# Two reorderings of one kernel at once: the tokenizer's taps tile by tile, and the attention's turns, table and tail

## The reference

```python
# 1 tokenizer, per image: 7 x 7 patches, 192 channels
loc = dwconv(gelu(conv(x, pl_w, stride=16)))          # depthwise 3x3, then 1x1
g = gelu(dwconv(gelu(conv(wavelet_packet(x), pg_w1))))
h = (1 - gate) * loc + gate * conv(g, pg_w2)
h = relu(dwconv(h, f1)); h = relu(dwconv(h, f2)); h = dwconv(loc + h, f3)
t = concat([cls, layernorm(tokens(h))]); h = concat([t, txt], 1)   # 32 x 82 x 192
# 2 selective scan (mamba): rmsnorm, z and gate, scan of 16 states, W_out, gated FFN
h = h + mamba(layernorm(h))
# 3 attention and experts
x = layernorm(h); x2 = ln(x)
x = x + out_proj(softmax(q k^T / 4) v)                # 12 heads
xm = ln(x); probs = softmax(xm @ router_w)            # 8 experts, the best 2 of each token
for e in range(8): out += combine[:, e] * (gelu(xm @ w1[e] + b1[e]) @ w2[e] + b2[e])
h = h + x + out
```

## Time and profile before

| | us |
|---|---|
| runs, median (lowest to highest) | 1427.9 (1424.58 to 1437.63) |
| the profiled execution | 1429.09 |
| its span | 1427.3 |
| PE / DVE / ACT / POOL busy | 1210.3 / 1022.4 / 705.8 / 777.2 |
| mean granted clock of TensorE, 1 is 2.4 GHz | 0.917 |

### The profile page before, as it was taken

One profiled execution on the slowest core, in us unless ns is written; L12 is line 12 of the kernel. 1 busy time (PEld: TensorE's weight loads), 2 busy tenths in 40 slices (PEclk: granted clock), 3 DMA queues, 4 the chain that ended last, 5 costly groups with the idle time before them and its releaser, 6 DMA issues.

```text
span 1427.3 us, 19317 instructions
## 1 busy us (share of the span) xinstructions
PE 1210.3 (85%) x5756; PEld 783.2 (55%) x5757; DVE 1022.4 (72%) x1935; ACT 705.8 (49%) x1490; POOL 777.2 (54%) x499
## 2 busy tenths in 40 slices
PE   6895745485999989898987799999999799999996
PEld 4342223242454545454552468888878577777775
DVE  3699886798999999899999746677776663333232
ACT  1137642476868676767766245555541332222221
POOL 3037895479687888869697320134443465222322
PEclk9797655699999999999999999999996699999998
DMA  5200000342404040403220001122221133222221
GB/s 177 57 1 0 30 9 29 118 126 79 142 1 142 1 142 1 141 28 114 90 83 0 1 21 48 42 63 57 58 67 55 36 58 55 35 38 37 35 37 20
...
## 3 DMA queue, kind: packets, MB, share of 16 engines
...
q10 hardware_dynamic: 2184, 1.72, 0.5%
...
## 4 chain that ended last, share of the span: by engine, by line
PE 52%; DVE 23%; issue 8%; ACT 8%; POOL 5%; DMA 3%; DVEq 0%; SPq 0%; POOLq 0%; ACTq 0%
PE ps L2137 10%; PE ps L2156 6%; PE ps L961 6%; DVE hs L1244 6%; DVE ps L180 5%; PE ps L1616 3%; PE ps L1559 3%; PE ps L872 3%; PE ps L2146 2%; ACT ps L1114 2%; PE ps L1629 2%; PE ps L938 2%; PE ps L897 2%; PE ps L915 2%; PE ps L875 2%
## 5 line engine op out<-in xcount | busy, mean ns | idle before, releaser
L1362 POOL TENSOR_TENSOR Bx<-dtz,Bb 128x984 f32<-128x984 f32 x128 | 289.4, 2281 | 43.5 <-DVE hs L1244 29.9
L1244 DVE TENSOR_TENSOR_SCAN hs<-ps,Bx 128x492 f32<-128x492 f32 x256 | 287.6, 1164 | 22.1 <-POOL Bx L1362 12.7
L1114 ACT ACTIVATE ps<-dt,A 128x324 f32<-128x324 f32 (+1 forms) x512 | 211.5, 456 | 78.0 <-DVE hs L1244 77.2
L961 PE MATMUL ps<-hs,b_id 128*128 128x492 f32 x512 | 236.4, 584 | 12.0 <-DVE y L1211 9.3
L2256 POOL DMA_INDIRECT out<-yt,dest x48 | 74.8, 1558 | 164.7 <-DVE yt L2242 156.3
L1254 DVE TENSOR_TENSOR hs<-hs,ps 128x984 f32<-128x984 f32 x128 | 150.2, 1174 | 2.5 <-issue 0.6
L2137 PE MATMUL ps<-W,xT 97*128 (+1 forms) x384 | 140.6, 509 | 4.1 <-ACT hb L2194 1.4
L961 PEld LDWEIGHTS ps<-hs,b_id 128*128 128x128 f32 x512 | 92.2, 193 | 79.1 <-issue 73.8
L2226 DVE COPY hT__5781<-ps 128x768 f32<-128x768 f32 x48 | 46.0, 958 | 112.6 <-PE ps L2146 110.0
L2005 POOL DMA_INDIRECT buckets<-XS,c_slot x64 | 90.9, 1421 | 36.5 <-issue 23.6
L2012 POOL TENSOR_TENSOR c_x<-c_x,bro 82x192 f32<-82x192 f32 x32 | 19.2, 599 | 167.0 <-DVE c_x L1801 166.8
...
## 6 DMA issues: line engine op xcount, KB each, us to landing
...
```

The lines of the kernel that those rows point to most:

```text
L961: mm = pe.matmul(ps[:, BANK_Y + h, 0:HALF], ident[:], f2(hs[:, s % LONG])[:, h * HALF:(h + 1) * HALF], start=s == 0, stop=s == STATE - 1)
L1114: a = act.activation(ps[:, BANK_A + h, c:c + w].rearrange("p (g t) -> p g t", t=S)[:, :, 1:S], dt[:, (par + t // STATE) % 2, m, g0 * S:g1 ...
L1244: v.tensor_tensor_scan(f2(hs[:, t % LONG])[:, c], ps[:, BANK_A + h, 0:HALF], f2(Bx[:, t % RING])[:, c], 0.0, ALU.mult, ALU.add).then_inc(s ...
L1362: g.tensor_tensor(Bx[:, t % RING], dtz[:, p], Bb[:, p, t % STATE, :].rearrange("p (a n) -> p a n", a=1).broadcast_to([128, NI, N]), ALU.mu ...
```

## The change

Two changes, timed here together.

1. Tokenizer. `s_conv` and `s_gelu` count tiles; PE's next `conv` starts a tile as soon as its PSUM tile is free, ACT's Gelu and DVE's taps start with the first tile. The wait for D1 (and for the DF tiles) moves behind the eighth tap. On DVE the last waves are in another order; `third_sums` of the last chunk writes DF[0] rather than DF[2], and its ninth tap waits for the reader of DF[0] (`last_read`). On ACT the scan's piece of the last wave goes behind the last products, on POOL the roots go behind the two PF adds.
2. Attention. The turn of the normed rows moves from the end of q = 0 to q = 1, between scores and product with V; on DVE the attention's own small operations go ahead of `normed`, `rank` and `pick`; reading the counts (`offsets`) is first in q = 1. The first table covers 12 tiles and needs 4 rounds; it is made in round 6, in three parts, and no longer in the tail. In the tail PE turns tiles 0 and 1 ahead of the first step, `up` of tile 0 goes ahead of the second and of tile 1 ahead of the third. Two rounds' normed rows get buffers of their own, cleared early by POOL. The scatter-adds into the output have four buffers rather than two, and stand three to a round's scatters.

```diff
-        def dw(eng, own, src, dst, tiles, c, col, done):
+        def dw(eng, own, src, dst, tiles, c, col, done, given=None, read=None):
 
             part = src.shape[0]
             acc = psF[0:part, 0:ROWS * GRID].rearrange("p (r c) -> p r c", c=GRID)
             for k in tiles:
+                if given is not None:
+                    eng.wait_ge(*given(k))
                 for t in range(9):
+                    if t == 8 and read is not None:
+                        eng.wait_ge(*read(k))
...
+        def last_sums(c):
+            return DF[0] if c == CH - 1 else DF[2]
+
+        def last_read(c):
+            return (s_f[0], CH) if c == CH - 1 else (s_f[2], c * FILLS)
...
-                if c >= 1:
-                    pe.wait_ge(s_gelu, c)
                 for t in range(3):
+                    if c >= 1:
+                        pe.wait_ge(s_gelu, 3 * (c - 1) + t + 1)
                     for k in range(KT):
                         mm = pe.matmul(psC[:, t, 0:NP], wc[:, k, t * 128:(t + 1) * 128], xc[:, c % 2, k, :],
                                        start=k == 0, stop=k == KT - 1)
-                mm.then_inc(s_conv, 1)
+                    mm.then_inc(s_conv, 1)
...
-                act.wait_ge(s_conv, c + 1)
                 if c == 0:
                     act.wait_ge(s_pad, 1)
                     act.wait_ge(s_padp, 1)
                 for t in range(3):
-                    i = act.activation(padded(P1, t, c), psC[:, t, 0:NP].rearrange("p (i r c) -> p i r c", i=IM, r=GRID),
-                                       ACT.Gelu, bias=vec[:, V_CONV_B + t:V_CONV_B + t + 1])
-                i.then_inc(s_gelu, 1)
+                    act.wait_ge(s_conv, 3 * c + t + 1)
+                    act.activation(padded(P1, t, c), psC[:, t, 0:NP].rearrange("p (i r c) -> p i r c", i=IM, r=GRID),
+                                   ACT.Gelu, bias=vec[:, V_CONV_B + t:V_CONV_B + t + 1]).then_inc(s_gelu, 1)
...
-                if w == WAVES - 1:
-                    tail("last wave")
...
+                if w == WAVES - 1:
+                    tail("last wave")
...
-            for w in range(WAVES):
+            def local_sums(w):
+
+                dw(v, own, P1, D1, range(3), w, V_DW, s_dw1, given=lambda k: (s_gelu, 3 * w + k + 1),
+                   read=(lambda k: (s_loc, w) if k == 0 else (s_g, w)) if w > 0 else None)
+
+            def first_sums(c):
+
+                v.wait_ge(s_h, c + 1)
+                dw(v, own, PF[0], DF[0], (0,), c, V_F_DW, s_dwf[0], read=(lambda k: (s_f[0], c)) if c > 0 else None)
+
+            def second_sums(c):
+
+                v.wait_ge(s_r1, c + 1)
+                dw(v, own, PF[1], DF[1], (0,), c, V_F_DW + 18, s_dwf[1], read=(lambda k: (s_f[1], c)) if c > 0 else None)
+
+            def third_sums(c):
+
+                v.wait_ge(s_lr, c + 1)
+                dw(v, own, PF[2], last_sums(c), (0,), c, V_F_DW + 36, s_dwf[2], read=(lambda k: last_read(c)) if c > 0 else None)
+
+            for w in range(CH + 1):
                 if w < CH:
-                    v.wait_ge(s_gelu, w + 1)
-                    if w > 0:
-                        v.wait_ge(s_g, w)
-                    dw(v, own, P1, D1, range(3), w, V_DW, s_dw1)
-                if 0 <= w - 1 < CH:
-                    v.wait_ge(s_h, w)
-                    if w > 1:
-                        v.wait_ge(s_f[0], w - 1)
-                    dw(v, own, PF[0], DF[0], (0,), w - 1, V_F_DW, s_dwf[0])
-                if 0 <= w - 5:
-                    norm_rows(w - 5)
-                if 0 <= w - 4:
-                    take_rows(w - 4)
-                if w == WAVES - 1:
-                    tail("last taps")
-                if 0 <= w - 2 < CH:
-                    v.wait_ge(s_r1, w - 1)
-                    if w > 2:
-                        v.wait_ge(s_f[1], w - 2)
-                    dw(v, own, PF[1], DF[1], (0,), w - 2, V_F_DW + 18, s_dwf[1])
-                if w == WAVES - 2:
-                    tail("last but one taps")
-                if 0 <= w - 3 < CH:
-                    c = w - 3
-                    v.wait_ge(s_lr, c + 1)
-                    if c > 0:
-                        v.wait_ge(s_f[2], c * FILLS)
-                    dw(v, own, PF[2], DF[2], (0,), c, V_F_DW + 36, s_dwf[2])
+                    local_sums(w)
+                if w >= 1:
+                    first_sums(w - 1)
+                if w == CH:
+                    take_rows(0)
+                if w >= 2:
+                    second_sums(w - 2)
+                if w >= 3:
+                    third_sums(w - 3)
+            second_sums(CH - 1)
+            norm_rows(0)
+            take_rows(1)
+            tail("last but one taps")
+            third_sums(CH - 2)
+            norm_rows(1)
+            third_sums(CH - 1)
+            take_rows(CH - 2)
+            tail("last wave")
+            tail("last taps")
...
-                if 0 <= w - 4:
-                    roots(w - 4)
...
+                if 0 <= w - 4:
+                    roots(w - 4)
...
-FIRST = 16
-FULL_ROUNDS = 5
+FIRST = 12
+FULL_ROUNDS = 4
...
-            return XS[:, p % 2] if p < ROUNDS - 1 else XS_last[:]
+            if p in (ROUNDS - 3, ROUNDS - 1):
+                return XS_more[p // 2 - (ROUNDS - 3) // 2][:]
+            return XS[:, p % 2] if p < ROUNDS - 3 else XS[:, 1]
...
+            def normed_rows(i):
+                pe.wait_ge(s_xn, i - 2 + 1)
+                turn(slots(i - 2), ("NT0", "NT1"), s_nt, i)
+
             def route(i, par, q):
-                if q == 0 and is_round(i - 2):
-                    pe.wait_ge(s_xn, i - 2 + 1)
-                    turn(slots(i - 2), ("NT0", "NT1"), s_nt, i)
...
+                if q == 1 and is_round(i - 2):
+                    normed_rows(i)
...
             program(pe, step, front, route=route)
             i, par = ROUNDS, ROUNDS % 2
+            t = ex.tensor(pe)
+            pe.wait_ge(s_L, ROUNDS - 2)
+            t.turn(0, 0)
+            pe.wait_ge(s_sl, ROUNDS - 3)
+            t.turn(1, 1)
+            step(i, par, 0)
             pe.wait_ge(s_e, 32 * EXPERTS)
-            t = ex.tensor(pe)
-            step(i, par, 0)
-            route(i, par, 0)
-            pe.wait_ge(s_PTa, ROUNDS * G)
-            t.turn(0, 0)
-            step(i, par, 1)
-            route(i, par, 1)
-            t.turn(1, 1)
             pe.wait_ge(s_tab, 1)
             pe.wait_ge(s_E, ROUNDS * G)
             t.up(0, 0, t.expert(0))
+            pe.wait_ge(ex.s_xT, 2)
+            step(i, par, 1)
+            route(i, par, 1)
+            t.up(1, 1, t.expert(1))
             step(i, par, 2)
             pe.wait_ge(s_PTv, ROUNDS * G)
             pe.wait_ge(s_x3, ROUNDS * G - 1)
-            t.step(0, 0)
+            t.flip(0, 0)
+            pe.wait_ge(s_PTa, ROUNDS * G)
+            t.turn(2, 0)
             pe.wait_ge(s_x3, ROUNDS * G)
             t.step(1, 1)
-            route(i + 1, 1 - par, 0)
+            normed_rows(i + 1)
             prefix(ROUNDS - 2)
             t.step(2, 2)
             route(i + 1, 1 - par, 1)
...
-                if q == 0 and is_round(i - 2):
-                    normed(i - 2, par)
-                if q == 0 and is_round(i - 3):
-                    rank(i - 3)
-                if q == 2 and is_round(i - 2):
...
+                if q == 0 and is_round(i - 2):
+                    normed(i - 2, par)
+                if q == 0 and is_round(i - 3):
+                    rank(i - 3)
                 if q == 1 and is_round(i - 3):
+                    offsets(i - 3)
                     gates(i - 3)
                     place(i - 3)
+                if q == 2 and i < ROUNDS and is_round(i - 2):
+                    pick(i - 2)
+                if i == FULL_ROUNDS + 2:
+                    if q == 1:
+                        full_tiles()
+                    if q == 2:
+                        which_experts(0, FIRST, le_full)
+                    if q == 3:
+                        which_rows(0, FIRST, le_full, None)
...
-                if is_round(p - 2) and p < ROUNDS - 1:
-                    v.wait_ge(s_sc, (p - 1) * (16 * 2 * G))
+                if p in (ROUNDS - 3, ROUNDS - 1):
+                    v.wait_ge(s_pad, 1 if p == ROUNDS - 3 else 2)
+                elif is_round(p - 2):
+                    v.wait_ge(s_sc, min(p - 1, FULL_ROUNDS) * (16 * 2 * G))
...
             i, par = ROUNDS, ROUNDS % 2
             t = ex.vector(v)
             t.ones()
-            full_tiles()
             step(i, par, 0)
             t.keep_tail(0, 0)
+            t.keep_tail(1, 1)
             step(i, par, 1)
-            t.keep_tail(1, 1)
             step(i, par, 2)
             norm(ROUNDS - 1, 1 - par, 3)
             rank(ROUNDS - 2)
-            v.memset(XS_last[:], 0.0).then_inc(s_last, 1)
+            t.step(0, 0)
+            normed(ROUNDS - 1, 1 - par)
             hb = H[:, (ROUNDS - 1) * G:B, :]
             v.tensor_tensor(hb, hb, XN[:, 1 - par], ALU.add).then_inc(s_add, 1)
```

(21 more changed lines are left out.)

123 lines of the change are left out of this document (63 added, 60 removed).

## The result

| | before | changed |
|---|---|---|
| median of 4 runs each, us | 1430.81 | 1386.43 |
| lowest to highest | 1424.58 to 1437.63 | 1381.22 to 1397.67 |
| span of the profiled execution | 1427.3 | 1388.6 |

The median before is over four runs here, over three (1427.9) ahead of the prediction. The ratio is 0.970, with a 95% interval of 0.962 to 0.978: 44 us faster by the medians, 38.7 by the two profiled executions. 1370 was expected, 59 less than the profiled execution; 1386.4 lies in the range (1354 to 1396). The direction and the places were right. Of the 59 us forecast, a quarter (by the medians) to a third (by the two profiled executions) did not come. The measured time lies above the 1362 to 1378 that the forecast had by itself; the range holds it because it took in the rivals, of which the first (clock at 1.2 GHz in round 7 and the tail) stood at 1385.

A forecast was written before the change was run, and what follows sets the result against it. DVE's waits were taken to count in the tokenizer, PE to bound the loop, the clock to matter in round 7 and tail. 26 + 8 + 11 + 14 = 59 us off 1429.1 gave 1370; range 1354 to 1396.

The forecast's parts named there:

- the first (clock at 1.2 GHz in round 7 and the tail): Round 7 and tail: rival that the clock stays low there, gaining 10 us instead of 25, 1385 us; chance 0.20.
- Head and wait for D1: Tokenizer: DVE's first tap comes 9.0 us earlier and its 12.75 us wait for D1 goes nearly whole, 12.7.
- What is late next: Tokenizer: ACT's products and POOL's adds move only 17.6 us, so DVE's wait for POOL's sum grows to some 7.7.
- Last waves: Tokenizer's end: the new order saves DVE 5.5 us for roots and 8.6 for the gate, less 3 beside POOL's adds.
- the walk's 28.7: Tokenizer: the step-by-step sum 17.6 + 14.1 − 3 = 28.7 us, of which 26 was taken for unseen small stalls.
- two more slow passes than I counted: Tokenizer's last waves: by the skill's contention rule two further passes would pay beside POOL's adds; one, about 3 us, was counted.
- Attention, rounds 2 to 6: Attention loop: PE's waits for XS and counts, 9.2 us, nearly vanish; 8 us taken, ends 3 and 9.5.
- The rival that the loop loses its clock: Attention loop: rival that rounds run at 1.2 GHz, 26 us more each, 1474 us with four; chance 0.03.
- Round 7: Last attention round: without PE's stand for XS the clock stays up and DVE sets the length; 11 us taken, ends 2 and 12.
- Tail: After round 7: the new order walks to 30 us from 48.30, a gain of 18; 14 taken, ends 8 and 18.
- Clock 0.5 behind the loop's last round: Round 7 and tail: a sign that, if seen, would show the forecast wrong; round 7 was expected at clock 1.00.
- Experts: Experts: the 12-tile table needs rows some 24 us earlier, costing nothing; up to 8 us if that cover is gone.

The follow-up runs named there:

- tok: Only the tokenizer's part of the change, attention and experts as before, against the kernel before; 1409.4 us, ratio 0.981.
- back: The changed kernel with the turn of XS in rounds 2 to 7 back at the end of q = 0, ahead of the scores; 1403.0 us, ratio 0.979.
- fill: The changed kernel with one extra unused wide matmul at two stands of PE, in round 7 and the tail; 1392.5 us, ratio 0.972.
- hand: The changed kernel with the old order of the last waves on DVE, ACT and POOL, handover by tiles kept; 1400.3 us, ratio 0.979.
- turn: The new tokenizer plus only the loop's share of the attention part (XS turn, DVE order, `offsets`), table, tail and buffers as before; 1396.0 us, ratio 0.975.
- again2: The changed kernel, unaltered, run a third time; 1387.9 us, ratio 0.970 to the kernel before.
- prod: The changed kernel with ACT's products of the first and second later stage ahead of the next chunk's Gelu in waves 1 to 3; 1381.7 us, ratio 0.967.
- again: The changed kernel, unaltered, run once more for another profile; 1386.0 us, ratio 0.967 to the kernel before.

## Why the prediction was right, and where it was too large

**Head and wait for D1 (9.0 and 12.7 us taken).** Right: 9.56 us in the profile, and the next chunk's taps follow without a wait. DVE was done with the second chunk's taps at 61.3 us, where it had been 82.9; 21.6 us ahead, and 21.7 was said.

**What is late next.** Right in kind: the chain over ACT's products and POOL's adds took over, and the wait grew, to 8.9 us where 7.7 was said, and to 14 us in those executions (tok, back, fill, hand, turn, again2) whose clock fell in the first wave, at 43 to 45 us. With the whole tokenizer's part, the three profiles without that fall have the first scan at 258.4 to 260.6, the five with it at 264.3 to 266.5. `prod` shows that this wait wasn't POOL's alone: ACT's order kept the products behind a Gelu whose input was late.

**Last waves.** `second_sums(3)` at 176.8 for 208.7, no wait for the roots, the gate's wait 4.5 for 8.6. I had counted one more pass beside POOL's adds at 3 us, and that is what came: two passes of `norm_rows` took 3.95 and 4.60 us, where one had been slow before. The scan's first copies, which had stood where POOL was idle, came beside the adds too:

```profile
197.34 0.94 DVE L1286 TENSOR_SCALAR wzg<-wzg 128x384 f32<-128x384 f32 x1
198.29 1.17 DVE L1287 TENSOR_SCALAR wzg<-wzg 64x384 f32<-64x384 f32 x1
199.50 1.92 DVE L1288 CAST sel<-oh 96x2048 bf16<-96x2048 f32 x1
```

Before, these three took 0.36, 0.36 and 1.22 us. In all some 5 us where 3 were taken. The gate gave 4.1 us, not 8.6, and the lead was 15.7, not 17.6. Against these misses stands one the other way: DVE's waits for the rows themselves (L308 before, L319 now), taken to stay, fell from 7.0 to 2.3 us. 15.7 + 5.5 + 4.1 − 4.9 + 4.7 = 25.1, and the first scan gained 24.45 of 26. That the share came so near is partly luck: the walk's 28.7 was off by more than 4 us, the discount to 26 took most of it, and the misses partly cancel. The Trainium skill, "SBUF — State Buffer", section "Who interferes with whom", had been cited against the order with two more slow passes than I counted. They didn't come: the last two passes of `norm_rows` stand where POOL is idle and take 1.40 and 1.39 us. Beside the adds the passes took about three times as long, as its rule about two inputs in SBUF would have it. By the same section `tensor_scalar` and `cast` can contend with GpSimd as well, in their two-port modes; the three rows are slower beside the adds, which agrees with that.

**Attention, rounds 2 to 6 (8 taken, 1.7 in the profile).** The mechanism was right: the waits went from 11.2 to 1.3 us (the 2.0 of round 7 included), a round without a fall takes 32.9 for 34.4, and in `fill`, with no fall in the loop, rounds 2 to 6 gained 7.4. The step that failed is "rounds 2 to 6 [...] I take 8 us": it took the clock as given. In ten profiles with the moved turn there are 11 falls in 40 rounds, each some 3 us, with PE busy all the time; the mean gain of the ten in rounds 2 to 6 is 4 to 5 us. The old place has one in 12 (at a stand of 1.7 us, in tok; one more in round 2 of back). The rival that the loop loses its clock was this mechanism, at a tenth of its price: the clock is back after 6.8 us.

**Round 7 (11 taken).** 19.3 us in five of ten profiles, a gain of 11.7; 22.6 to 26.2 in the others. By the mean of 21.7, against 31.7 of the three with the turn at the old place, 10 us. "If PE doesn't stand there it keeps its clock" holds half the time. In the first profile PE still stands 0.93 us there:

```profile
1050.01 1.82 PE L1638 MATMUL ps<-kB,qT 128*82 128x328 f32 x8
1052.76 0.77 PE L1573 MATMUL ps<-b_id,XS 82*96 82x82 f32 x8 [0.93 <-DVE XS L1879]
1053.36 1.94 PE L1653 MATMUL ps<-V,PT 82*82 82x17 f32 x24
1055.14 0.49 PE L1660 MATMUL ps<-b_id,ao 82*96 82x82 f32 x2
1055.42 1.85 PE L1667 MATMUL ps<-b_id,E 82*82 82x82 f32 x12
```

but it does so for 0.92 us in `again` too, whose clock stays up. So this stand doesn't decide it by itself. Whether it makes a fall likelier isn't shown: behind the moved turn the clock fell in 11 of 40 loop rounds without a stand and in 5 of 10 rounds 7.

**Tail (14 taken, 7.3 in the profile).** By the mean of the new tails but fill's, 40.1 against 49.2, 9 us; and the rest grew by 2 to 3 us: in the first profile 9.3 us lie between `up` of tile 3 and of tile 4, for 7.0 before, with this `up` partly at half clock (4.10 us for 2.85). Net 6; `turn` says 4 to 8. The failed step is the clock again: the 14 were taken as if the tail kept its clock. PE's work in the tail is 34.86 × 0.75 = 26.1 us at full clock in the profile, as forecast (26.3); with the 5.9 us of idle it has there it would take 32. The difference to 40.8 is half clock. I had this as a rival for tail and round 7 together, with chance 0.20; in the tail the clock falls in every profile (means of 0.64 to 0.86), in round 7 in half of the new ones. "Clock 0.5 behind the loop's last round" was one of my signs of being wrong, and it came. The total, 1386, is that rival's 1385; the gain of round 7 and tail, 14.6 us in the first profile, lies between its 10 and the forecast's 25.

**Experts.** No load of tile 12 held PE up: the only idle behind 1112 us is 2.4 us of `up` [issue] and 0.8 for yb. The cover held.

So of the 20.3 us that the profile fell short of 59, 1.5 lie in the tokenizer, 6.3 in the loop and just ahead of it, 3.6 in round 7, 6.7 in the tail and 2.2 behind it. Those in loop, round 7 and tail are matters of the clock. The 2.2 lie between `up` of tiles 3 and 4: some 1.7 are `up` and `flip` partly at half clock, the rest a longer idle time ahead of tile 4.
